# Edge attention of a graph network: the order of copy, selection and turning inside the merged group loop

## The chip, the cores and the metric

The kernel runs on one core of one Trainium2 chip. The metric is the device time of one execution in microseconds (us), lower is better. The engines that matter here are TensorE (PE, with its weight loads PEld), VectorE (DVE), ScalarE (ACT), GpSimd (POOL), which issues the gathers, and SyncE (SP), which issues the plain transfers. They run their own instruction streams in order and wait for one another on semaphores.

## What is computed

A graph with 6250 nodes and 100000 edges, sorted by their target node, goes through four network blocks, each with a residual connection and a layer norm. The first three (a graph convolution, a mean aggregation, five edge layers with batch norm) take the first 72% of the time and are not touched. The change lies in the fourth, two attention convolutions of this form (heads H = 4, channels C = 32 each):

```
def _transformer_conv(x, src, dst, ea, Wq, bq, Wk, bk, Wv, bv, We, Ws, bs, H, C):
    q = (x @ Wq + bq).reshape(n, H, C)
    k = (x @ Wk + bk).reshape(n, H, C)
    v = (x @ Wv + bv).reshape(n, H, C)
    e = (ea @ We).reshape(-1, H, C)
    kj = k[src] + e
    vj = v[src] + e
    alpha = jnp.einsum('ehc,ehc->eh', q[dst], kj) / jnp.sqrt(jnp.asarray(C, x.dtype))
    amax = jax.ops.segment_max(alpha, dst, num_segments=n)
    p = jnp.exp(alpha - amax[dst])
    denom = jax.ops.segment_sum(p, dst, num_segments=n)
    w = p / denom[dst]
    msg = (vj * w[..., None]).reshape(-1, H * C)
    out = jax.ops.segment_sum(msg, dst, num_segments=n)
    return out + x @ Ws + bs
```

## The kernel before

**Groups.** The edges are laid out in tiles of 128 that each belong to one window of 128 target nodes. Four tiles are a group (`GROUP`), and there are 208 groups (`GROUPS`) in a convolution. Rings of four buffers (`RING`) hold gathered rows, index columns and selection matrices; buffer `g` is group `q` modulo 4. Every loop is written with four groups in its body. `_converse` is the function that the change touches; it runs twice, once in each convolution, and `_attend` finishes the last 64 groups after it.

**Two jobs.** For each group the kernel (a) scores its edges and (b), later, adds its weighted messages to their targets. Job (a), "look", goes through these steps, written here with their lines:
- `index` (ScalarE, L701 to L704) copies the source numbers of a group into `idx`. It waits until the group four back has been scored (`joined`) and its value half has been written to DRAM (`spilled`).
- GpSimd (L692) issues four indirect DMAs, one for each tile, that gather the rows of keys and values into `gbuf` (`bigDE`). SyncE stores the value half to DRAM (L649, `walk_value`).
- `select` (ScalarE, L706 to L712) draws the 0/1 matrices that say which edge has which target in the window: four `Abs` (L709) and one `Relu` (L712). It waits until the group four back has been asked.
- `turned_to` (TensorE, L798) transposes the four matrices into PSUM (`turned`, two buffers).
- the copy (ScalarE, L721) brings them back to SBUF (`turn`, two buffers).
- `ask` (TensorE, L807) multiplies them with the queries of the window, which gives each edge its target's query in PSUM (`part`, two buffers). Ahead of it TensorE loads four window numbers into registers (L563).
- VectorE: `tell` (L886), `multiply` (L891, waits for the gather), `reduce` (L896), `finish` (L901).

**Job (b)** starts once a span of groups has been scored and the maxima of its softmax are known. The spans are 40, 48, 56 and 64 groups long (`SPANS`). For a group `p` of the span before:
- SyncE loads its values back (L655, `walk_value` to `rings`); `blend` (VectorE, L923) multiplies them with the weights into `msg`.
- `extend` (ScalarE, L734 and L735) puts two more sets of columns beside them. It waits for the scatter of the group two before its own.
- the marks, which edge has which target, are drawn by ScalarE for even groups (`draw`, L726 and L729) and by VectorE for odd ones (`mark`, L912).
- `scatter` (TensorE, L822) multiplies marks and messages, in two halves; VectorE adds the results to the nodes (`add`, L932).

**Stages of `_converse`.** Looking at span 0 alone (40 groups). Then, for each k = 1, 2, 3: eight "fresh" groups (`FRESH`), each a look and then a part of the serial softmax work of span k - 1 (`soft_part`, small steps that pass between VectorE, TensorE and ScalarE); then the merged loop, in which each step looks at a group of span k and adds a group of span k - 1: 40, 48 and 56 steps. Here the names in one step q are: it looks at group q and scatters group q' = q - SPANS[k].

**The order in one merged step** is written by hand, engine by engine. ScalarE: `extend` for q' + 1, then `look` (`index` for q + 2, `select` for q + 1, the copy for q), then on even groups `draw` for q' + 2. TensorE: `turned_to` q, `ask` q, `scatter` q'. VectorE: `tell`, `multiply`, and then `reduce`, `finish`, `mark` and `blend` for q' + 1 between the four adds. `_hold` is a wait; `Gate.at(n)` is the semaphore's value after n events.

Of the kernel before, what the change touches and what calls it, by code (L numbers as in the profile page):

```python
# [19 lines left out]
GROUP = 4  # L20
# [552 lines left out]
def _converse(c, table, query, agg, odd, score, spill, dram, x, skip, offset, spare, weights=()):  # L573
# [65 lines left out]
    with nc.psum_tensor(c.name("part"), [P, 2, GROUP, 2 * P], F32) as part, \  # L639
# [59 lines left out]
        def _(e):  # L699
# [14 lines left out]

            def look(i, g):
                q = i * RING + g
                index(i + (g + 2) // RING, (g + 2) % RING)
                select(q + 1, (g + 1) % RING)
                _hold(e, c.product, q - 1, c.tick_act)
                e.wait_ge(c.turned.sem, c.turned.at(q + 1))  # L720
                e.activation(turn[:, g % 2, :, :], turned[:, g % 2, :, :], ACT.Copy).then_inc(c.message.sem, 1)  # L721

            def draw(q, g):
                e.wait_ge(c.scattered.sem, c.scattered.at(2 * (q - RING + 1)))
# [33 lines left out]
            for q in range(2):  # L758
                index(0, q)
            select(0, 0)  # L760
            with _loop(e, *rounds(0)) as i:
                for g in range(RING):
                    look(i, g)
            for k in range(1, last + 1):
                begin, end = rounds(k)
                for n in range(FRESH):
                    look(begin + n // RING, n % RING)
                    soft_part(k - 1, n)
                if k == 1:
                    draw(0, 0)  # L770

                def steps(i, final):
                    for g in range(RING):
                        q = i * RING + (g - SPANS[k])
                        if not (final and g == RING - 1):
                            extend(k - 1, q + 1, (g + 1) % RING)
                        look(i, g)
                        if g % 2 == 0:
                            draw(q + 2, (g + 2) % RING)
                e.wait_ge(c.lined.sem, c.lined.at(step(k, 0)))  # L780
                extend(k - 1, STARTS[k - 1], 0)
                with _loop(e, begin + FRESH // RING, end - 1) as i:
                    steps(i, False)
                steps(end - 1, True)
# [7 lines left out]
        def _(e):  # L792
# [59 lines left out]
            def skipped(chunks):  # L852
                for n in chunks:
                    e.wait_ge(c.chunked.sem, c.chunked.at(n - 3))
                    e.matmul(skips[:, n % 4, 0:CHUNK], c.W3[:, c.parts[3]:c.parts[3] + D],
                             x[:, n * CHUNK:(n + 1) * CHUNK], start=True, stop=True).then_inc(c.applied.sem, 1)
            with _loop(e, *rounds(0)) as i:
                for g in range(RING):
                    turned_to(i, g)
                    ask(i, g)  # L860
            for k in range(1, last + 1):
                begin, end = rounds(k)
                for n in range(FRESH):
                    turned_to(begin + n // RING, n % RING)
                    ask(begin + n // RING, n % RING)
                    soft_part(k - 1, n)
                with _loop(e, begin + FRESH // RING, end) as i:
                    for g in range(RING):
                        turned_to(i, g)
                        ask(i, g)  # L870
                        scatter(i - SPANS[k] // RING, g)
            soft_part(last, 0)
            e.wait_ge(c.joined.sem, c.joined.at(GROUPS))
# [8 lines left out]
        def _(e):  # L882
# [194 lines left out]
                steps(end - 1, True)  # L1077
            for n in range(FRESH):
                soft_part(last, n)
    for gate in (c.product, c.turned, c.joined, c.message, c.scored):  # L1080
        gate.passed(GROUPS)
    c.keyed.passed(2 * GROUPS)
    c.select.passed(GROUPS + 1)
    c.near.passed((GROUPS + 1) * GROUP)
    c.index.passed(GROUPS + 2)
    for g in c.gathered:
        g.passed(16 * GROUP * ROUNDS)
# [1240 lines left out]
```

## Time and profile before

| What | us |
| --- | --- |
| median of 3 runs | 11971.59 |
| lowest and highest | 11969.77, 11971.92 |
| the profiled execution's own time | 11962.17 |
| its span in the profile | 11960.3 |

Busy over the whole span: PE 74%, PEld 56%, DVE 63%, ACT 53%, POOL 64%. In the last 12 of the page's 40 slices, which hold the two attention convolutions, PE, DVE, ACT and POOL are each busy between 30 and 70% of the time, and none of them is the plain bound. The reader should not ask there which engine has the largest share, but which wait ends last in a step. The mean granted TensorE clock is 0.851 of full speed for the whole kernel and lower in the convolutions, where it moves between its two levels, 1.2 and 2.4 GHz.

### The profile page before, as it was taken

To read this page: it belongs to the slowest core of one execution; us is meant where nothing else is said; L and a number is where in the kernel's file an instruction comes from. 1 tells how busy PE (TensorE), PEld (TensorE's weight loads), DVE (VectorE), ACT (ScalarE), POOL (GpSimd) and SP (SyncE) were. 2 spreads that over 40 slices of the span, in tenths; PEclk is the share of its full clock that TensorE was granted. 3 is DMA by queue.
4 is the path that set the end of the run, shared out by engine and by line. 5 is a ranking of instruction groups with operands and counts; after the bars stand their busy time and mean duration, and the time that the engine had idled before them with its cause. 6 is when DMAs were issued, how large, how long until landed. Compare 5 with 4: busy or idle time off the path is not lost. (4 is left out here: it accounts for less than half of the span.)

```text
span 11960.3 us, 289382 instructions
## 1 busy us (share of the span) xinstructions
PE 8826.2 (74%) x56131; PEld 6641.4 (56%) x56132; DVE 7580.9 (63%) x21898; ACT 6379.7 (53%) x16860; POOL 7683.9 (64%) x7879
## 2 busy tenths in 40 slices
PE   5887788788688868877886888688755555555555
PEld 2776677466455545555564555455445555445554
DVE  5777777555567767666766676667644445544446
ACT  4544444544455555555555555555555555455554
POOL 2777777677677757757775775677365554565553
PEclk7998899799799989998998999899866667666677
DMA  2111111222244434434443443444254444454443
GB/s 56 32 31 33 34 31 29 65 56 56 73 111 111 109 97 110 111 91 116 111 111 94 110 111 83 125 110 112 85 155 140 144 140 126 124 149 141 140 144 100
DMA packets 1311535, 1169.02 MB, mean 98 GB/s; under 512 B 239258, under 2 KB 1106238, under 8 KB 1310224
## 3 DMA queue, kind: packets, MB, share of 16 engines
q0 software_dynamic: 272544, 566.00, 18.5%
q1 hardware_dynamic: 1038256, 596.28, 17.3%
q14 instruction: 647, 5.30, 0.1%
q8 instruction: 88, 1.44, 0.1%
HBM read 1009.04 MB, written 152.40 MB: 97 GB/s over the span
## 5 line engine op out<-in xcount | busy, mean ns | idle before, releaser
L1407 POOL DMA_INDIRECT rings<-rows_key,idx x4536 | 4365.3, 962 | 1908.7 <-issue 1330.4
L1591 DVE TENSOR_TENSOR bigDE<-bigDE,part 128x128 f32 (+1 forms) x6656 | 1891.8, 284 | 1390.1 <-PE part L1502 408.9
L692 POOL DMA_INDIRECT bigDE<-rows_key_value,idx x1664 | 1627.9, 978 | 1343.4 <-ACT idx L704 731.4
L1502 PE MATMUL part<-rings 128*128 128x128 f32 (+1 forms) x11920 | 1713.3, 290 | 648.2 <-ACT rings L1443 248.0
L1515 PE MATMUL wide<-bigDE,bigC 128*128 128x384 bf16 x10800 | 1943.3, 337 | 250.3 <-DVE bigC L1573 238.8
L1502 PEld LDWEIGHTS part<-rings 128*128 128x128 f32 (+1 forms) x11920 | 1560.6, 190 | 821.7 <-issue 743.7
L1434 ACT ACTIVATE rings<-iota,relK 128x128 f32<-128x128 f32 x5960 | 1900.3, 389 | 4.9 <-issue 1.5
L1407 POOL DMA_INDIRECT rings<-rows_hidden,idx x1424 | 1377.8, 968 | 595.7 <-issue 408.7
L1426 ACT COPY idx<-srcK 128x4 int32 (+1 forms) x1490 | 283.6, 191 | 2498.8 <-PE part L1502 2324.4
L1515 PEld LDWEIGHTS wide<-bigDE,bigC 128*128 128x128 bf16 x10800 | 1069.5, 101 | 984.4 <-issue 390.0
L807 PE MATMUL part<-bigB,rings 128*128 x3328 | 741.1, 390 | 1076.0 <-ACT rings L721 1072.4
L1573 DVE TENSOR_SCALAR bigC<-bigC,node 128x512 bf16<-128x512 int16 x4410 | 1384.2, 379 | 45.1 <-issue 42.5
L807 PEld LDWEIGHTS part<-bigB,rings 128*128 128x128 f32 x3328 | 625.0, 277 | 1220.5 <-issue 1220.5
L1515 PE MATMUL wide<-bigF,bigC 128*128 128x384 bf16 x6840 | 1169.7, 326 | 174.6 <-DVE bigC L1573 172.1
L1437 ACT ACTIVATE rings<-rings,ones 128x512 f32<-128x512 f32 x1490 | 1075.6, 722 | 48.4
L1541 DVE TENSOR_TENSOR rings<-rings 128x512 f32<-128x512 f32 x945 | 654.6, 693 | 650.1 <-DMA rings<-rows_key,idx 624.7
L1515 PEld LDWEIGHTS wide<-bigF,bigC 128*128 128x128 bf16 x6840 | 654.3, 98 | 615.0 <-issue 204.0
L1515 PE MATMUL wide<-bigDE,rings 128*128 128x192 bf16 x9408 | 898.0, 253 | 108.4 <-DVE rings L1573 104.4
L1515 PEld LDWEIGHTS wide<-bigDE,rings 128*128 128x128 bf16 x9408 | 801.3, 101 | 176.6 <-issue 162.5
L886 DVE TENSOR_TENSOR bigDE<-part,wK 128x16 f32<-128x16 f32 x416 | 72.6, 175 | 1208.6 <-PE part L807 1208.5
L1573 DVE TENSOR_SCALAR rings<-W,node 128x512 bf16<-128x512 int16 x2352 | 743.4, 381 | 35.0 <-issue 34.9
L1443 ACT ACTIVATE rings<-rings 128x512 f32<-128x512 f32 x945 | 586.0, 620 | 316.8 <-DVE rings L1541 314.1
(372 smaller groups left out, 11296.6 us busy)
## 6 DMA issues: line engine op xcount, KB each, us to landing
rings<-in_attr SPq DMA_DIRECT2D x3780, 64.0 KB
walk_value<-bigDE SPq DMA_DIRECT2D x416, 256.0 KB, 2.5
rings<-walk_value SPq DMA_DIRECT2D x416, 256.0 KB
rings<-rows_key,idx POOLq DMA_INDIRECT x4536
bigDE<-rows_key_value,idx POOLq DMA_INDIRECT x1664
bigF<-in_attr SPq DMA_DIRECT2D x380, 64.0 KB
rings<-rows_hidden,idx POOLq DMA_INDIRECT x1424
rows_key<-rings SPq DMA_DIRECT2D x60, 320.0 KB, 2.6
```

The source lines that it names most:

```text
L692: e.indirect_dma_start(gbuf[:, g, r, :], None, table, bass.IndirectOffsetOnAxis(ap=c.idx[:, g, r:r + 1], axis=0)).then_inc(c.gathered[g].s ...
L807: done = e.matmul(part[:, g % 2, r, 0:D + HEADS], turn[:, g % 2, r, :], query[:, bass.ds(where[r] * (D + HEADS), D + HEADS)], start=True, ...
L1407: e.indirect_dma_start(to[:, r, 0:width], None, table, bass.IndirectOffsetOnAxis(ap=idx[:, r:r + 1], axis=0)).then_inc(gate.sem, 16)
L1426: e.copy(to, c.srcK[:, bass.ds(q_of(i, n) * GROUP, GROUP)]).then_inc(c.index.sem, 1)
L1434: e.activation(to[:, r, :], c.iota[:, :], ACT.Abs, bias=c.relK[:, bass.ds(q * GROUP + r, 1)], scale=-1.0).then_inc(c.near.sem, 1)
L1437: e.activation(to, to, ACT.Relu, bias=c.ones[:, 0:1], scale=-1.0).then_inc(c.select.sem, 1)
L1443: e.activation(x, x, ACT.Relu).then_inc(c.message.sem, 1)
L1502: last = e.matmul(part[0:width, bank(n), r, :], msg[:, r, 0:width], sel[:, r, :], start=True, stop=True)
L1515: last = e.matmul(wide[:, r, 0:3 * width], hot[:, r * P:r * P + P], room.pieces(s, 1).rearrange("p a j f -> p (a j f)"), start=s == 0, sto ...
L1541: e.tensor_tensor(to, to, plus, ALU.add).then_inc(c.joined.sem, 1)
L1573: e.tensor_scalar(hots[(half * NODE_TILES + s) % depth], room.sources[half], c.node[:, s:s + 1], None, ALU.is_equal).then_inc(c.hot.sem, 1)
L1591: e.tensor_tensor(into, into, got, ALU.add).then_inc(c.added.sem, 1)
```

## The change

In `_converse` alone:
- ScalarE: in `look` the copy of group q comes first; after it `index` for q + 2 and then `select`, which is now for q + 2 where it was for q + 1. Before the first loop there is one more `select`, for group 1. In a merged step the whole `look` now stands ahead of `extend`.
- TensorE: turning runs one group ahead. Group 0 is turned before the first loop; then every step is `ask` q, `turned_to` q + 1, and after that the soft part or the scatter.
- The counts that the semaphores have reached at the end grow by one: one group more is turned, and one group more is selected, at the end.

```
             def look(i, g):
                 q = i * RING + g
-                index(i + (g + 2) // RING, (g + 2) % RING)
-                select(q + 1, (g + 1) % RING)
                 _hold(e, c.product, q - 1, c.tick_act)
                 e.wait_ge(c.turned.sem, c.turned.at(q + 1))
                 e.activation(turn[:, g % 2, :, :], turned[:, g % 2, :, :], ACT.Copy).then_inc(c.message.sem, 1)
+                index(i + (g + 2) // RING, (g + 2) % RING)
+                select(q + 2, (g + 2) % RING)
...
             select(0, 0)
+            select(1, 1)
...
                         q = i * RING + (g - SPANS[k])
+                        look(i, g)
                         if not (final and g == RING - 1):
                             extend(k - 1, q + 1, (g + 1) % RING)
-                        look(i, g)
                         if g % 2 == 0:
                             draw(q + 2, (g + 2) % RING)
...
+            def following(i, g):
+                turned_to(i + (g + 1) // RING, (g + 1) % RING)
+            turned_to(0, 0)
             with _loop(e, *rounds(0)) as i:
                 for g in range(RING):
-                    turned_to(i, g)
                     ask(i, g)
+                    following(i, g)
...
                 for n in range(FRESH):
-                    turned_to(begin + n // RING, n % RING)
                     ask(begin + n // RING, n % RING)
+                    following(begin + n // RING, n % RING)
                     soft_part(k - 1, n)
                 with _loop(e, begin + FRESH // RING, end) as i:
                     for g in range(RING):
-                        turned_to(i, g)
                         ask(i, g)
+                        following(i, g)
                         scatter(i - SPANS[k] // RING, g)
...
-    for gate in (c.product, c.turned, c.joined, c.message, c.scored):
+    for gate in (c.product, c.joined, c.message, c.scored):
         gate.passed(GROUPS)
+    c.turned.passed(GROUPS + 1)
     c.keyed.passed(2 * GROUPS)
-    c.select.passed(GROUPS + 1)
-    c.near.passed((GROUPS + 1) * GROUP)
+    c.select.passed(GROUPS + 2)
+    c.near.passed((GROUPS + 2) * GROUP)
```

ScalarE's row in the last round of the first merged loop, where it stands without register instructions, before. L734 and L735 are `extend`, L704 `index`, L709 and L712 `select`, L721 the copy:

```order
L734 COPY bigC<-bigF 128x4x4
L735 COPY bigC<-bigC 128x4x4
L704 COPY idx<-srcK 128x4
L709 ACTIVATE rings<-iota,relK 128x128 x4
L712 ACTIVATE rings<-rings,ones 128x512
L721 ACTIVATE rings<-turned 128x512
L726 ACTIVATE rings<-iota,relK 128x128 x4
L729 ACTIVATE rings<-rings,ones 128x512
```

The same step of the changed kernel; L719 is the copy here:

```order
L719 ACTIVATE rings<-turned 128x512
L704 COPY idx<-srcK 128x4
L709 ACTIVATE rings<-iota,relK 128x128 x4
L712 ACTIVATE rings<-rings,ones 128x512
L734 COPY bigC<-bigF 128x4x4
L735 COPY bigC<-bigC 128x4x4
L726 ACTIVATE rings<-iota,relK 128x128 x4
L729 ACTIVATE rings<-rings,ones 128x512
```

The copy went from the sixth place to the first, and `extend` from the first to the fifth, ahead of `draw` (L726, L729).

TensorE's row in the first merged loop before, from the turning of a group (L798) over the loading of the window numbers (L563) to the first matmul of `ask` (L807), and then from its last to the scatter (L822):

```order
L798 MATMUL turned<-ident,rings 128x128 x4
L563 ISA
L563 TENSOR_LOAD nRow
L186 REGISTER_ALU
L805 REGISTER_ALU
L807 ISA
L807 MATMUL part<-bigB,rings 128x132
...
L820 ISA
L822 MATMUL halves<-bigC,rings 128x136 x2
L820 REGISTER_ALU
L822 MATMUL halves<-bigC,rings 128x136 x2
```

The same place in the changed kernel, from the last matmul of `ask` (L808 here) over the turning (L799) and the scatter (L823) to the loading of the next window numbers:

```order
L808 MATMUL part<-bigB,rings 128x132
L186 REGISTER_ALU
L797 REGISTER_ALU
L799 MATMUL turned<-ident,rings 128x128 x4
L186 ISA x2
L186 REGISTER_ALU
L821 ISA
L823 MATMUL halves<-bigC,rings 128x136 x2
L821 REGISTER_ALU
L823 MATMUL halves<-bigC,rings 128x136 x2
L563 ISA
L563 TENSOR_LOAD nRow
```

Turning moved from ahead of `ask` to between `ask` and the scatter, and what it turns is the next group.

## Rows read from the trace of the kernel before

**Rows 1.** Busy time by stage; columns: stretch, length, engines' busy time, clock, DMA

```profile
core 0: us, PE busy (x) PEld busy (x) DVE busy (x) ACT busy (x) POOL busy (x), PEclk, DMA share, GB/s
8656.50:8849.00 192.50, 98.60 (x464) 84.31 (x464) 68.62 (x161) 102.34 (x273) 145.12 (x155) 0.65 0.60 163
8904.80:9186.50 281.70, 171.05 (x799) 154.66 (x798) 134.72 (x381) 151.88 (x451) 154.76 (x159) 0.70 0.50 146
...
sum 2037.90, PE 1229.13 PEld 1112.76 DVE 965.46 ACT 1098.52 POOL 1088.76; mean PE 204.86 PEld 185.46 DVE 160.91 ACT 183.09 POOL 181.46
...
9186.50:9250.40 63.90, 29.58 (x121) 24.04 (x122) 32.60 (x78) 26.71 (x72) 37.24 (x35) 0.54 0.45 129
...
sum 367.70, PE 174.58 PEld 142.77 DVE 191.97 ACT 163.49 POOL 226.37; mean PE 29.10 PEld 23.79 DVE 32.00 ACT 27.25 POOL 37.73
```

**Rows 2.** Timeline of one merged step and a half, in order of time

```profile
start us, us, engine line op out<-in xcount [idle before <-releaser]
9331.85 0.20 ACT L734 COPY bigC<-bigF 128x16 f32 x1 [4.12 <-PE halves L822]
9332.33 0.19 ACT L704 COPY idx<-srcK 128x4 int32 x1
9333.33 0.94 POOL L692 DMA_INDIRECT bigDE<-rows_key_value,idx  x1 [2.21 <-ACT idx L704]
...
9334.48 0.58 ACT L721 ACTIVATE rings<-turned 128x512 f32<-128x512 f32 x1
9334.95 1.26 ACT L726 ACTIVATE rings<-iota,relK 128x128 f32<-128x128 f32 x4
...
9335.43 2.12 PE L807 MATMUL part<-bigB,rings 128*128 x8 [3.29 <-ACT rings L721]
9336.25 0.72 ACT L729 ACTIVATE rings<-rings,ones 128x512 f32<-128x512 f32 x1
9337.35 2.02 PE L822 MATMUL halves<-bigC,rings 128*128 128x136 f32 x8
9339.16 1.06 PE L798 MATMUL turned<-ident,rings 128*128 128x128 f32 x4
9339.49 0.20 ACT L734 COPY bigC<-bigF 128x16 f32 x1 [2.52 <-PE halves L822]
```

**Rows 3.** Who waited for whom in the first merged loop, 40 steps

```profile
engine line waited for: us in total, times, longest us
DVE bigDE L886 <- PE part L807: 128.8, 41, 4.2
PE part L807 <- ACT rings L721: 109.6, 40, 3.3
POOL bigDE L692 <- ACT idx L704: 86.2, 38, 2.9
```

**Rows 4.** Timeline of the looking stage without merged work

```profile
8747.46 0.19 ACT L704 COPY idx<-srcK 128x4 int32 x1 [2.35 <-DMA walk_value<-bigDE]
8748.51 0.94 POOL L692 DMA_INDIRECT bigDE<-rows_key_value,idx  x1 [0.30 <-issue]
8749.76 0.94 POOL L692 DMA_INDIRECT bigDE<-rows_key_value,idx  x1 [0.30 <-issue]
...
8753.87 0.69 DVE L891 TENSOR_TENSOR bigDE<-bigDE,part 128x512 f32<-128x512 f32 x1 [0.93 <-DMA bigDE<-rows_key_value,idx]
```

**Rows 5.** Timeline of VectorE's operations beside GpSimd's gathers, merged and fresh

```profile
9340.61 0.68 DVE L923 TENSOR_TENSOR bigC<-rings,bigF 128x512 f32<-128x512 f32 x1
9340.91 1.20 POOL L692 DMA_INDIRECT bigDE<-rows_key_value,idx  x1 [2.90 <-ACT idx L704]
...
9207.22 1.82 DVE L935 TENSOR_TENSOR_SCAN bigF<-bigF,small,bigC 128x768 f32<-128x768 f32 x1
...
9207.75 2.04 POOL L692 DMA_INDIRECT bigDE<-rows_key_value,idx  x1 [0.30 <-ACT idx L704]
```

**Rows 6.** Timeline of fresh groups of span 2, and who waited there

```profile
9190.66 1.06 PE L798 MATMUL turned<-ident,rings 128*128 128x128 f32 x4
...
9194.35 2.12 PE L807 MATMUL part<-bigB,rings 128*128 x8 [2.62 <-ACT rings L721]
...
DVE bigDE L886 <- PE part L807: 25.1, 8, 9.1
```

More of the change, by code:

```diff
@@ L716, in look @@
                 q = i * RING + g
-                index(i + (g + 2) // RING, (g + 2) % RING)
-                select(q + 1, (g + 1) % RING)
                 _hold(e, c.product, q - 1, c.tick_act)
@@ L721, in look @@
                 e.activation(turn[:, g % 2, :, :], turned[:, g % 2, :, :], ACT.Copy).then_inc(c.message.sem, 1)
+                index(i + (g + 2) // RING, (g + 2) % RING)
+                select(q + 2, (g + 2) % RING)
             def draw(q, g):
@@ L760, in _ @@
             select(0, 0)
+            select(1, 1)
             with _loop(e, *rounds(0)) as i:
@@ L774, in steps @@
                         q = i * RING + (g - SPANS[k])
+                        look(i, g)
                         if not (final and g == RING - 1):
                             extend(k - 1, q + 1, (g + 1) % RING)
-                        look(i, g)
                         if g % 2 == 0:
@@ L856, in skipped, with following @@
                              x[:, n * CHUNK:(n + 1) * CHUNK], start=True, stop=True).then_inc(c.applied.sem, 1)
+            def following(i, g):
+                turned_to(i + (g + 1) // RING, (g + 1) % RING)
+            turned_to(0, 0)
             with _loop(e, *rounds(0)) as i:
                 for g in range(RING):
-                    turned_to(i, g)
                     ask(i, g)
+                    following(i, g)
             for k in range(1, last + 1):
@@ L863, in _ @@
                 for n in range(FRESH):
-                    turned_to(begin + n // RING, n % RING)
                     ask(begin + n // RING, n % RING)
+                    following(begin + n // RING, n % RING)
                     soft_part(k - 1, n)
@@ L868, in _ @@
                     for g in range(RING):
-                        turned_to(i, g)
                         ask(i, g)
+                        following(i, g)
                         scatter(i - SPANS[k] // RING, g)
@@ L1079, in _ @@
                 soft_part(last, n)
-    for gate in (c.product, c.turned, c.joined, c.message, c.scored):
+    for gate in (c.product, c.joined, c.message, c.scored):
         gate.passed(GROUPS)
+    c.turned.passed(GROUPS + 1)
     c.keyed.passed(2 * GROUPS)
-    c.select.passed(GROUPS + 1)
-    c.near.passed((GROUPS + 1) * GROUP)
+    c.select.passed(GROUPS + 2)
+    c.near.passed((GROUPS + 2) * GROUP)
     c.index.passed(GROUPS + 2)
```

## The prediction

> **What bounds the kernel now.** First I cut the two convolutions into stages by the busy-time view [rows 1]. The six merged loops (40, 48 and 56 steps, twice) last 2037.90 us for 288 steps, 7.08 us a step. The six fresh stages last 367.70 us for 48 groups. In the plain looking stage a group takes about 5 us. No engine fills a merged step: from the first loop's row, per step, PE is busy 171.05 / 40 = 4.3 us, DVE 3.4, ACT 3.8, POOL 3.9. So a chain of waits sets the 7.08 us, and the timeline shows it [rows 2]. The scatter ends and releases ScalarE at 9331.85; ScalarE does `extend`, index, selection and then the copy (L721 at 9334.48, 0.58 us); TensorE has waited 3.29 us for that and asks at 9335.43; the scatter follows at 9337.35 and releases ScalarE at 9339.49. That is 7.64 us once around, at the lower TensorE clock. Of it 3.58 us (9331.85 to 9335.43) is ScalarE's part, in which TensorE stands still after its turning; the rest is ask 1.92, scatter 2.02 and 0.12 to the next row. The waits say the same in sums [rows 3]: TensorE waited for the copy 109.6 us in 40 steps, 2.74 each; VectorE for the ask 128.8; GpSimd 86.2 for an index column, 2.2 each, since index stands behind the same release.
>
> **The change, part by part.**
>
> *The copy ahead of index, selection and extend.* Group q is now turned before the scatter of the step ahead, so the copy finds its input early. What lay between scatter and ask, 3.58 us, leaves the path: the copy runs beside the scatter, and the ask needs only the scatter's end and a copy done before. Index and selection (together 9332.33 to 9334.48, 2.15 us) stay on ScalarE but are wanted one step later (the turning of q + 2 is in the next step). What is queued behind the copy's wait: index, select, extend, draw. `extend` still waits for the scatter of the step before, and behind it in ScalarE's queue are `draw` on even groups (L726 and L729, 9334.95 to 9336.97, 2.02) and the next copy. That is the one chain left between the two: 0.12 + 0.48 (extend, 9331.85 to 9332.33) + 2.02 + 0.58 + 0.37 = 3.6 us from a scatter's end to an ask, in the worst step. At the lower clock TensorE works longer than that between a scatter's end and the next scatter's end, and at the higher one the chain spans two steps, so it doesn't bind.
>
> *What is late next.* Each engine's own work in a step, run without a stop. TensorE at the lower clock [rows 2]: ask 1.92, scatter 1.81 (9337.35 to 9339.16), turning 0.85 (its 1.06 less the tail that overlaps): 4.6 us; less at the higher one. ScalarE: 9331.85 to 9334.48, 2.63, the copy to the next operation 0.47, and half a draw 1.01: 4.1 us. VectorE: 3.4 busy plus the gaps between dependent adds, at most 4.3. GpSimd: four gathers of 0.94 with 0.30 of issue between them (8748.51 to 8749.76 is 1.25 [rows 4]): 5.0 us. So GpSimd is the next bound. The looking stage shows that it can run so: there every gather follows the last after 0.30, though ScalarE waits 2.35 us for a store before each index column [rows 4], because index is two groups ahead. A merged step keeps that lead: from index column to gather start is 1.0 us (9332.33 to 9333.33), four gathers take 5.0, landing some 2 more, 8 us in all, and the multiply that wants them is two steps, 10 us or more, behind.
>
> *The hold on GpSimd.* A gather that starts while VectorE runs a certain kind of operation is stretched: beside L923 it took 1.20 instead of 0.94 and ended 0.82 after L923 did (9340.61 + 0.68 + 0.82 = 9342.11 = 9340.91 + 1.20); beside the scan L935 it took 2.04 and ended 0.75 after it [rows 5]. Now the idle time of GpSimd hides this; with GpSimd as the bound it counts. A step has one L923 and, every second time, one mark L912 of the same size, 0.68. A start comes each 1.25 us, falls into an operation with chance 0.68 / 1.25 = 0.54 and is held half of it, 0.34: 0.19 for each operation, 0.28 a step. The ends are 0 (starts fall beside them) and 0.82 (mark and blend together, 1.29 us, held in full every second step, half a blend in the others). I take 0.28, because the stretched rows now lie between the ends too. Hence 5.28 us a step, between 5.0 and 5.8. The Trainium skill, page "SBUF — State Buffer", section "Who interferes with whom", agrees that a VectorE operation with two SBUF inputs blocks GpSimd's reads, but infers that such a tensor_tensor does not stall descriptor generation; by that the step would be 5.0 and the sum 81 us lower. The row of 1.20 us speaks against the inference, so I don't take it.
>
> *Merged loops:* 288 x 5.28 = 1521 against 2038: **-517 us** (5.0: -598; 5.8: -367).
>
> *Turning ahead in the fresh stages.* There TensorE comes out of a soft part, turns (9190.66), waits 2.62 for the copy and asks at 9194.35 [rows 6]; with the matrices already turned and copied it asks where it now turns, up to 3.7 us earlier. VectorE waits 25.1 us for asks in a stage; the longest, 9.1, is mostly softmax work on ScalarE that stays (I count 2 of it for index and selection), and in the others the part caused by turning and copy is 1 to 3 us. I take 11 us of the 64 in a stage, 66 for six; 78 if all others go; 40 if GpSimd, whose eight groups need 8 x 5 = 40 us and more under scans [rows 5], binds first, as it may in the two stages of 55 us. **-66 us.**
>
> *Looking stages:* nothing, they are GpSimd's already [rows 1, 4]. *Added work:* one selection (2.0 us) before and one behind the loops, and one turning (0.9) before the last scatter, in each convolution. The first hides behind the first gathers, the last behind the final softmax work. I charge 2 us. More traffic in a shorter step: the DMA share, now 0.50, becomes 0.50 x 7.08 / 5.28 = 0.67, near the 0.60 at which the looking stage already runs without a pause.
>
> **Sum.** Profiled execution 11962.2 (1.9 of it outside the span) - 517 - 66 + 2 = 11381. The median of the runs lies 9.4 above the profiled one: 11391, say **11390**. Bounds: 11962 + 9 - 598 - 78 = 11295, and 11962 + 9 + 2 - 367 - 40 = 11566.
>
> **The rivals.**
> - *The chain only gets shorter.* ScalarE's row in order (extend behind the scatter, draw, copy) still stops TensorE, or registers and waits cost more than I see: for a step of 6 to 6.8 us. For it speaks that TensorE's 4.6 us leaves little slack at the lower clock. Time: 288 x (7.08 - 6.4) = 196, with half the fresh gain 33: 11742. Range 11570 to 11860.
> - *It doesn't do what it says.* If the copy always waited for a turning that is held back by its own selection, ask would come no earlier. Against: that selection was made a step before. Time 11970.
> - *Slower: index too late.* Index is now behind the copy, and the copy waits for TensorE. If gathers land more than two steps after their index column (8 us now; with the copy's 0.6 and doubled landing still 11), VectorE waits for gathers that now are in time. It decides only when that latency passes 2 x 7.08 = 14.2 us; at 16 the step is 8.0: 288 x 0.9 = 260 us more, 12230. Against: the looking stage bears higher traffic per us with no such growth.
>
> **How the numbers follow.** Forecast 0.82 (11295 to 11566), shorter chain 0.11, no effect 0.03, slower 0.04. The range 11295 to 11570 leaves out somewhat under 0.2. A measurement here tells 0.2% (24 us) from no change. Faster by more: 0.82 + 0.11 = 0.93, less a rounding for the mildest of the chain cases: 0.92; within 0.2%: 0.04; slower: 0.04.
>
> **What would show it.** Right: merged loops of 200 to 230 us for 40 steps instead of 282; gathers with 0.30 between them and some of 1.2 to 1.6 us; no wait of TensorE for the copy of near 3 us; VectorE waiting for gathers, not for asks; ScalarE waiting at index, as in the looking stage. If instead GpSimd still waits for index columns, the chain has only been shortened; if most of the gathers are stretched, the hold is larger than I took it. If the fresh stages stay at 64, the softmax chain alone sets them. The TensorE clock doesn't enter the forecast; it would if TensorE became the bound.

## The result and the profile after

| What | us |
| --- | --- |
| changed kernel, median of 4 runs | 11327.85 |
| lowest and highest | 11314.04, 11329.24 |
| kernel before beside it, median of 4 runs | 11971.76 |
| ratio, 95% interval | 0.946 (0.9443 to 0.9476) |
| profiled execution of the changed kernel | 11327.94 (span 11326.1) |

The changed kernel is 5.4% faster, 644 us by the medians and 634 by the two profiled spans (11960.3 and 11326.1). The forecast was 11390, with 11295 to 11570 as its range: the time lies in the range, and the gain is 63 us larger than forecast.

The page of the changed kernel: busy time of each engine, and the groups of the gathers and of `ask` (busy, mean ns of one, idle time ahead of them and its cause).

```profile
PE 8557.2 (76%) x56134; PEld 6362.2 (56%) x56140; DVE 7582.3 (67%) x21898; ACT 6355.2 (56%) x16870; POOL 7714.8 (68%) x7879
...
L692 POOL DMA_INDIRECT bigDE<-rows_key_value,idx x1664 | 1647.3, 990 | 692.0 <-issue 654.3
...
L808 PE MATMUL part<-bigB,rings 128*128 x3328 | 678.2, 366 | 358.8 <-ACT rings L719 236.8
```

TensorE's idle time ahead of `ask` that is put down to the copy was 1072.4 us in all 416 groups before (109.6 of it in the 40 steps of [rows 3]). It is 236.8 us now, and only 7.1 of that lies in the six merged loops. What stands ahead of a gather is no longer a wait for an index column: 654.3 of 692.0 us is `issue`, the 0.30 us between one gather and the next.

The stages of the first convolution after, cut as in [rows 1]: looking, fresh, merged, fresh, merged. Behind them stand the sums of all six merged loops and of all six fresh stages.

```profile
core 0: us, PE busy (x) PEld busy (x) DVE busy (x) ACT busy (x) POOL busy (x), PEclk, DMA share, GB/s
8670.10:8862.60 192.50, 100.11 (x468) 86.31 (x468) 68.80 (x160) 100.92 (x272) 145.02 (x154) 0.64 0.59 162
8862.60:8916.20 53.60, 31.66 (x128) 26.66 (x129) 29.24 (x65) 31.46 (x86) 41.60 (x40) 0.50 0.57 163
8916.20:9113.80 197.60, 132.55 (x786) 114.84 (x784) 135.43 (x380) 146.75 (x442) 150.07 (x153) 0.86 0.70 202
9113.80:9170.60 56.80, 32.46 (x133) 27.12 (x134) 32.95 (x76) 28.62 (x79) 42.29 (x40) 0.52 0.57 160
9170.60:9408.40 237.80, 162.38 (x948) 140.12 (x946) 162.63 (x456) 179.40 (x537) 181.01 (x186) 0.83 0.70 203
...
sum 1430.60, PE 949.40 PEld 822.62 DVE 970.63 ACT 1062.99 POOL 1086.84; mean PE 158.23 PEld 137.10 DVE 161.77 ACT 177.17 POOL 181.14
...
sum 331.40, PE 175.97 PEld 146.83 DVE 191.97 ACT 174.77 POOL 252.10; mean PE 29.33 PEld 24.47 DVE 31.99 ACT 29.13 POOL 42.02
```

Against [rows 1]: merged loops 2037.9 to 1430.6, 607.3 less, 4.97 us a step where it was 7.08; fresh stages 367.7 to 331.4, 36.3 less; the looking stage 192.5 both times. GpSimd's busy time in the merged loops did not change (1088.8 and 1086.8): it is the same work, packed into less time, 76% of it. TensorE's fell from 1229 to 949 with a granted clock of 0.83 to 0.87 where it was 0.70 in the first row.

Nearly the whole gain stands in one row, that of the gathers (busy, mean ns | idle ahead of them). These are the 832 gathers of the first convolution, the kernel before first and the changed one second. Each row also holds 73 us of idle time ahead of the first gather.

```profile
L692 POOL DMA_INDIRECT bigDE<-rows_key_value,idx x832 | 814.6, 979 | 660.0 <-ACT idx L704 366.4 <-issue 293.5
...
L692 POOL DMA_INDIRECT bigDE<-rows_key_value,idx x832 | 822.9, 989 | 334.5 <-issue 313.2 <-ACT idx L704 21.2
```

Busy and idle together are 1474.6 us before and 1157.4 after: 317.2 less. From the first gather to the last, the second convolution is 315.0 us shorter (1397.7 and 1082.7). The two make 632 us. From the last gather to the last multiplication it is another 6 and 5 us shorter (10.5 before, 4.4 and 5.1 after), and 13 are lost ahead of the first gather (8641.8 before, 8655.0 after), where the change touches nothing: 631 of the 634 us between the spans. A run of 208 groups without a pause, 5.0 us each (1.25 a gather [rows 4]), would be 1040 us; the changed kernel needs 1084: 1040, 37 of stretched gathers, 8 of pauses. In the kernel before the pauses are 334 us, counted in the same way.

The timeline of a merged step and a half of the changed kernel. L895 is `multiply`, L905 `finish`, L916 `mark`, L927 `blend`, L719 the copy.

```profile
9299.84 0.69 DVE L916 TENSOR_TENSOR rings<-relK,iota 128x512 f32<-128x512 f32 x1
...
9300.31 1.04 POOL L692 DMA_INDIRECT bigDE<-rows_key_value,idx  x1 [0.30 <-issue]
9300.81 0.69 DVE L927 TENSOR_TENSOR bigC<-rings,bigF 128x512 f32<-128x512 f32 x1 [0.28 <-DMA rings<-walk_value]
...
9302.15 0.19 ACT L704 COPY idx<-srcK 128x4 int32 x1 [1.26 <-DVE bigF L905]
...
9302.47 0.34 SPq L655 DMA_DIRECT2D rings<-walk_value  x1
...
9303.79 2.12 PE L808 MATMUL part<-bigB,rings 128*128 x8 [0.81 <-issue]
...
9306.44 0.69 DVE L927 TENSOR_TENSOR bigC<-rings,bigF 128x512 f32<-128x512 f32 x1 [2.50 <-DMA rings<-walk_value]
9306.66 1.29 POOL L692 DMA_INDIRECT bigDE<-rows_key_value,idx  x1 [0.30 <-issue]
9306.77 0.57 SPq L649 DMA_DIRECT2D walk_value<-bigDE  x1
9306.80 0.60 ACT L719 ACTIVATE rings<-turned 128x512 f32<-128x512 f32 x1 [0.36 <-PE turned L799]
```

TensorE asks (9303.79) without waiting for a copy; in [rows 2] it had waited 3.29 us. ScalarE waits at its index column, and GpSimd doesn't wait at all. Who waited for whom in the second merged loop of 48 steps, and, in the last row, the same for SyncE's own queue:

```profile
PEld halves L823 <- DVE bigDE L936: 68.3, 45, 3.2
PE halves L823 <- DVE bigDE L936: 55.1, 44, 3.0
POOL bigDE L692 <- issue: 54.7, 178, 0.7
DVE bigC L927 <- DMA rings<-walk_value: 52.2, 42, 2.5
ACT idx L704 <- DVE bigF L905: 34.8, 30, 2.6
...
SPq L649 <- DMA bigDE<-rows_key_value,idx: 170.6, 47, 5.7
```

In this stage no compute engine waits for a gather directly. SyncE does, 170.6 us of 237.8: its store of a group waits for that group's gathers, and the reload of values for the scatter (L655) stands behind the store in the same queue. By the trace's landing events the gathers of one group were in at 9306.61; the store went out at 9306.77, the reload behind it at 9307.60, and its data were in at 9311.40; the next `blend` started at 9311.67. VectorE waits for the reload, TensorE's scatter for VectorE's adds. This is how a late gather reaches the other engines. It doesn't show by itself that GpSimd sets the pace. In the second merged loop of the kernel before (342.4 us), where GpSimd was not the bound, SyncE waited for gathers even longer:

```profile
SPq L649 <- DMA bigDE<-rows_key_value,idx: 270.0, 48, 7.5
```

What names GpSimd is its own row: 8 us of pauses in 1084.

### The profile page after: what moved, and what is told of

The parts are those of the page before. It is cut to its first block and busy times, and to the rows that moved or that the text cites. A ratio compares the mean times of both kernels' runs of the same rounds, so it can differ in the third digit from the quotient of the medians.

```text
span 11326.1 us, 289319 instructions
## 1 busy us (share of the span) xinstructions
PE 8557.2 (76%) x56134; PEld 6362.2 (56%) x56140; DVE 7582.3 (67%) x21898; ACT 6355.2 (56%) x16870; POOL 7714.8 (68%) x7879
## 5 line engine op out<-in xcount | busy, mean ns | idle before, releaser
L692 POOL DMA_INDIRECT bigDE<-rows_key_value,idx x1664 | 1647.3, 990 | 692.0 <-issue 654.3
L1439 ACT ACTIVATE rings<-iota,relK 128x128 f32<-128x128 f32 x5960 | 1900.2, 389 | 4.9 <-issue 1.5
L808 PE MATMUL part<-bigB,rings 128*128 x3328 | 678.2, 366 | 358.8 <-ACT rings L719 236.8
L808 PEld LDWEIGHTS part<-bigB,rings 128*128 128x128 f32 x3328 | 583.1, 260 | 454.3 <-issue 453.7
L709 ACT ACTIVATE rings<-iota,relK 128x128 f32<-128x128 f32 x1680 | 536.5, 390 | 0.0
```

Of the source, the lines that this page charges most:

```text
L692: e.indirect_dma_start(gbuf[:, g, r, :], None, table, bass.IndirectOffsetOnAxis(ap=c.idx[:, g, r:r + 1], axis=0)).then_inc(c.gathered[g].s ...
L709: e.activation(c.sel[:, g, r, :], c.iota[:, :], ACT.Abs, bias=c.relK[:, bass.ds(q * GROUP + r, 1)], scale=-1.0).then_inc(c.near.sem, 1)
L808: done = e.matmul(part[:, g % 2, r, 0:D + HEADS], turn[:, g % 2, r, :], query[:, bass.ds(where[r] * (D + HEADS), D + HEADS)], start=True, ...
L1439: e.activation(to[:, r, :], c.iota[:, :], ACT.Abs, bias=c.relK[:, bass.ds(q * GROUP + r, 1)], scale=-1.0).then_inc(c.near.sem, 1)
```

## The experiments

Two theories were to be told apart. **GpSimd's run**: once the copy no longer stands behind the scatter, a convolution lasts as long as 832 gathers of 1.25 us, their holds and pauses. **The shorter chain**: the order of the engines still sets the step, only with fewer links. Under each kernel stands its row of the 832 gathers of the first convolution. Busy and idle in it add up to a sum that is 1157.4 for the changed kernel; twice the difference is what the first theory gives for the kernel's time.

### ScalarE's part alone, TensorE's part alone

The first kernel turns a group right ahead of its `ask`, as before, and keeps the rest of the change:

```
+                    turned_to(i, g)
                     ask(i, g)
-                    following(i, g)
                     scatter(i - SPANS[k] // RING, g)
```

> The changed kernel, but TensorE turns a group right ahead of its ask, as before; only ScalarE's new order is kept. Theory (GpSimd is the new bound, and both halves of the change were needed at the lower TensorE clock only): behind a scatter's end now stand turning 0.85, copy 0.6, two hand-overs of 0.15 and 0.37, ask 1.9 and scatter 1.8, 5.7 us a merged step at 1.2 GHz and under 5.0, GpSimd's time, at 2.4 GHz: 5.1 to 5.7 us a step, 11350 to 11550 us in all. Rival (turning ahead is what gives the gain): merged steps stay near 7 us and the time near 11970.

Measured: 11357.97 us, ratio 0.9493 (0.9477 to 0.9509), in the range of the theory.

The second keeps TensorE's part and gives ScalarE its old order:

```
                         q = i * RING + (g - SPANS[k])
-                        look(i, g)
                         if not (final and g == RING - 1):
                             extend(k - 1, q + 1, (g + 1) % RING)
+                        look(i, g)
...
             def look(i, g):
+                index(i + (g + 2) // RING, (g + 2) % RING)
+                select(q + 1, (g + 1) % RING)
...
-                index(i + (g + 2) // RING, (g + 2) % RING)
-                select(q + 2, (g + 2) % RING)
```

> The changed kernel, but ScalarE does extend, index, select (one ahead) and copy in the order of before; only TensorE turns ahead. Theory: nothing is gained in the merged loops, since the copy still stands behind extend, index and select, which stand behind the scatter; and the turning, which was hidden while TensorE waited, now stands between ask and scatter: 7.1 to 7.9 us a step, 11950 to 12220 us in all. Rival (turning was on the path): 6.2 us a step, 11700.

Measured: 12179.45 us, ratio 1.018 (1.0163 to 1.0197), in the range of the theory. The gathers of the first kernel and of the second, then a merged step and the first merged loop (columns as above) of the second:

```profile
L692 POOL DMA_INDIRECT bigDE<-rows_key_value,idx x832 | 823.7, 990 | 352.8 <-issue 314.7 <-ACT idx L704 38.1
...
L692 POOL DMA_INDIRECT bigDE<-rows_key_value,idx x832 | 812.9, 977 | 768.7 <-ACT idx L704 477.1 <-issue 291.6
...
9106.02 0.20 ACT L734 COPY bigC<-bigF 128x16 f32 x1 [5.32 <-PE halves L822]
...
9107.46 0.94 POOL L692 DMA_INDIRECT bigDE<-rows_key_value,idx  x1 [3.62 <-ACT idx L704]
...
9108.52 0.58 ACT L721 ACTIVATE rings<-turned 128x512 f32<-128x512 f32 x1
...
9109.52 2.12 PE L807 MATMUL part<-bigB,rings 128*128 x8 [3.65 <-ACT rings L721]
...
8903.60:9216.00 312.40, 175.18 (x793) 165.41 (x792) 134.60 (x380) 151.65 (x451) 152.29 (x159) 0.65 0.44 131
```

The gain is ScalarE's order: alone it brings 607 us (11964.8, the kernel before beside it, to 11358.0). TensorE's part alone costs 215. Its row shows why: from the scatter's release (9106.02) over `extend`, index, selection and copy to `ask` it is still 3.50 us, the same chain as in [rows 2], and the turning (9103.00 in the same trace, between `ask` and scatter) now lengthens the part that leads to the next release. A step is 7.8 us in this loop, 8.1 in the third. With ScalarE's part in place, turning ahead brings 30 us: the first kernel's gathers row is 19.1 longer, 38 in two convolutions.

### Selection one group ahead; extend first

Two links of the change taken back one at a time: `select(q + 1, ...)` in place of `select(q + 2, ...)`, and in the merged step `extend` ahead of `look` as before, with the order inside `look` left as changed.

> The changed kernel, but the selection runs one group ahead, as before, and no selection stands ahead of the first loop: copy q, index q+2, select q+1. Theory: the chain copy, index, select, turning (0.6 + 0.2 + 2.0 + 0.35 + 0.85 = 4.0 us) is shorter than GpSimd's 5.0, so the merged step stays at 5.0 and the whole within 0.3% of the changed kernel (11328). Rival (the second group of lead carries part of the gain): a step of 5.3 us or more, 11410 or more.

> The changed kernel, but ScalarE does extend ahead of look in the merged loops, as before; look itself has the copy first, and TensorE turns ahead. Theory: the copy stands behind the scatter again, but only with extend between: 0.12 + 0.48 + 0.58 + 0.37 + ask 1.92 + turning 0.85 + scatter 1.81 = 6.1 us a merged step at 1.2 GHz and 4.0 at 2.4 GHz, so GpSimd's 5.0 hides it at the higher clock: 5.1 to 6.0 us a step, 11360 to 11600. Rival (only index and selection had to leave the chain): no more than 0.2% over 11328.

Measured: 11321.59 us (0.946, 0.9444 to 0.9476), and 11332.48 us (0.9469, 0.9453 to 0.9485). Sums of their gathers rows: 1159.3 and 1163.8, so +4 and +13 us by the theory. Neither can be told from the changed kernel. For the first its theory was right. For the second the rival was right and the theory wrong: it had put the merged step at 5.1 to 6.0 us and the time at 11360 or more, and the steps are 5.00 to 5.13 us, where the changed kernel has 4.94 to 5.10. What counts is the order inside `look`: copy first, so that neither index nor selection stands between a scatter and an `ask`.

### Three gathers of four

One of a group's four gathers is left out, so a quarter of the edges are scored with stale rows. Store and `multiply` wait for three gathers then.

```
-                    for r in range(GROUP):
+                    for r in range(GROUP - 1):
                         e.indirect_dma_start(gbuf[:, g, r, :], None, table,
```

> The changed kernel with three of each group's four gathers; the fourth is left out, so a quarter of the edges are scored with stale rows. Theory (GpSimd sets the merged step and the looking stages): GpSimd needs 3.75 us a group, and the next bound comes up, TensorE and the waits around it, 3.8 to 4.5 us in a merged step; 11328 - 288 x 0.6 - 2 x 30 = about 11090 us. Rival (a chain sets the step, and GpSimd only happens to be as long): 5.0 us a step, 11300.

Measured: 10882.44 us, one execution. The first two merged loops, here of 40 and 48 steps:

```profile
8846.60:9004.30 157.70, 115.84 (x803) 99.41 (x801) 133.35 (x381) 146.51 (x455) 116.85 (x119) 0.96 0.76 227
9056.30:9243.10 186.80, 135.13 (x963) 114.58 (x961) 160.59 (x456) 176.15 (x547) 141.62 (x143) 0.99 0.77 228
```

Steps of 3.94 and 3.89 us, where three gathers of 1.25 take 3.75. Everything else in a merged step can be done in 3.9 us at the clock granted here, so in the changed kernel's 4.97 the other engines have slack, and the gathers are the bound. (At the lower clock, with the 4.6 us that the prediction counts for TensorE, the slack would be smaller.) I had expected 11090, with another engine binding at a longer step. The granted clock, 0.96 to 0.99 here, may be what took TensorE out of that; no run tested it. This run decides for GpSimd's run. It also takes traffic away, so one may ask whether the transfers were the bound and not GpSimd. They were not: with three gathers 227 and 228 GB/s are moved, at a DMA share of 0.76 and 0.77, where the changed kernel moves 202 and 203 at 0.70. The fresh stages stayed at 46 to 55 us (53 to 58 in the changed kernel): there something else holds too.

### Index one group ahead; longer fresh stages

The pipe's depth, and what VectorE's work in the fresh stages costs. In the first kernel the index column is made one group ahead; in the second VectorE has two extra reductions of some 3.3 us in each of the six fresh stages, 40 us in all.

```
-                index(i + (g + 2) // RING, (g + 2) % RING)
+                index(i + (g + 1) // RING, (g + 1) % RING)
...
                 if n == 2:
+                    if k < last:
+                        e.tensor_reduce(c.stats[:, 0, 0:24], c.iota[:, :].unsqueeze(1).to_broadcast([P, 24, P]),
+                                        AX.X, ALU.add)
```

> The changed kernel, but the index column is copied for the next group, not for the one after it, and only one stands ahead of the first loop: GpSimd's lead is one group. Theory (GpSimd runs without a stop through the whole of _converse because two groups are ready when a softmax step holds everything up): the lead, now 6 us of 10 in the merged loops, becomes about 1, GpSimd stops in the fresh stages for some 8 to 12 us each and a little in the merged loops: 11390 to 11480 us. Rival (one group of lead is enough): within 0.2% of 11328.

> The changed kernel with two more VectorE operations in each of the six fresh stages (sums over 3072 elements that nobody reads, about 3.3 us each, one in the parts 2 and 4 of the softmax work). Theory A (the fresh stages are under GpSimd too, which never waits in them; their length on VectorE is given back in the merged loop behind them): at most 10 us more than the changed kernel, 11328 to 11340. Theory B (fresh stages and merged loops add up, as the prediction counted them): 6 x 6.6 = 40 us more, 11365.

Measured: 11385.94 us (0.9512, 0.9496 to 0.9528), and 11341.1 us (0.9474, 0.9458 to 0.949). Their gathers rows, in this order:

```profile
L692 POOL DMA_INDIRECT bigDE<-rows_key_value,idx x832 | 818.2, 983 | 368.9 <-issue 311.5 <-ACT idx L704 57.5
...
L692 POOL DMA_INDIRECT bigDE<-rows_key_value,idx x832 | 818.2, 983 | 352.2 <-issue 312.6 <-ACT idx L704 39.6
```

Index one ahead costs 58 us, and the row gives 59 (1187.1 against 1157.4, twice). By the stages 39 us of it arise in the fresh stages, which are 59 to 64 us long, against 53 to 58, and 21 in the merged loops, with steps of 5.04 to 5.13. The theory's lower bound was 11390.

The second kernel is 13 us slower, 26 by the row; theory A had allowed 10 and theory B said 40. But the run tests less than it was meant to. VectorE is busy 38 us longer in the six fresh stages (230.5 against 192.0), and they are only 12.4 us longer (343.8 against 331.4), so most of the added work went into time in which VectorE had been idle. The merged loops gave nothing back; they are 15.7 us longer (1446.3 against 1430.6). Why, the lead shows, which is how many groups GpSimd has issued ahead of `multiply`. It is 1.5 at the start of a fresh stage in both kernels; at the end it is 2.75 to 3.5 in the changed kernel and 2.0 to 2.5 in this one. So a fresh stage isn't a term of its own: what it costs is what it makes GpSimd pause, and the merged loop behind it is longer or shorter by the lead that it hands over.

### The marks in another form

VectorE draws the marks of odd groups with four `tensor_scalar` in place of one `tensor_tensor`, to see whether the kind of operation holds the gathers.

```
-                e.tensor_tensor(marks[:, g, :, :], (relK, broadcast), (iota, broadcast), ALU.is_equal)
+                for r in range(GROUP):
+                    done = e.tensor_scalar(marks[:, g, r, :], c.iota[:, :], c.relK[:, bass.ds(q * GROUP + r, 1)],
+                                           None, ALU.is_equal)
```

> The changed kernel; VectorE draws the marks of odd groups with four tensor_scalar operations (one SBUF input and a scalar column each) in place of one tensor_tensor with two SBUF inputs. Theory (operations with two SBUF inputs hold a gather that starts under them): the mark's part of the stretched gathers goes, 0.15 us a merged step becomes 0.10 or less, 10 to 20 us in all: 11305 to 11320. Rival (tensor_scalar holds GpSimd as well, for as long as it runs): no fewer stretched gathers, 11325 to 11360.

> The changed kernel with both small edits: selection one group ahead, as before the change, and the marks of odd groups drawn by four tensor_scalar instead of one tensor_tensor. On a chip where GpSimd issues without a pause (gathers land some 2 us after their issue, as in the first profiles), the hold theory expects 11300 to 11320, some 10 to 15 us under the changed kernel's 11328, with holds of about 30 us in a convolution instead of 37, and the selection to make no difference. If the earlier 11315 of the marks alone was only a difference between chips, this gives 11320 to 11335 and the holds tell nothing. On a chip where gathers land some 10 us after their issue, as in the last three runs, GpSimd waits for index columns and the holds are covered: then this lies within 1% of the kernel before, 0.985 to 0.995 of it, and says nothing on the marks.

Measured: 11315.32 us (0.9451, 0.9435 to 0.9466) for the marks alone; 11320.67 us (11298.91 to 11322.12; 0.9453, 0.9441 to 0.9466) with selection one ahead as well. The first, then the second:

```profile
L692 POOL DMA_INDIRECT bigDE<-rows_key_value,idx x832 | 816.5, 981 | 330.9 <-issue 309.4 <-ACT idx L704 21.6
...
L692 POOL DMA_INDIRECT bigDE<-rows_key_value,idx x832 | 814.0, 978 | 332.7 <-issue 307.7 <-ACT idx L704 25.1
```

The holds go from 37 to 30 and 28 us in a convolution: busy time is 6.4 and 8.9 us lower than 822.9. By the sums of the rows alone that says little, since the two kernels of the section before have the old marks and 818.2. Over both convolutions 160 gathers are longer than 1.1 us in the changed kernel, 113 and 97 in these two, and 141 to 159 in the experiments above that have the old marks and all four gathers and take 11320 to 11390 us.

But this doesn't show that it takes two SBUF inputs to hold a gather. Of the 138 gathers that start beside a `tensor_scalar` of the new marks in the first kernel, 85 end 0.81 or 0.82 us after it, just as beside the old mark. They lose little, 0.08 us at most, because one such operation takes 0.28 us where the old mark takes 0.69. So the rival is right that `tensor_scalar` holds a gather too, and the long holds are fewer because each operation is short.

By the first theory the kernels should be some 20 us faster (sums 1147.4 and 1146.7, twice the difference to 1157.4); they are 13 and 7 us of 11328, with intervals that overlap that of the changed kernel. The profiled executions reach the first gather, up to which all these kernels are alike, anywhere between 8637 and 8659 us, so the time decides nothing of this size. A version that beats the changed kernel isn't shown by this.

### The same kernels on another chip

Three kernels (the changed one, with the new marks, with both edits) ran on another chip, on which the kernel before takes 14965.6 us.

> The changed kernel itself, run beside the next two, so that differences of 0.1% can be read on one chip: 11315 to 11330 us.

> The kernel with the marks drawn by tensor_scalar, again, beside the changed one. Theory (each operation with two SBUF inputs costs GpSimd what it holds): 10 to 15 us under the changed kernel, since the holds fell by 13 us in the first look. Rival (that was chance between executions): no difference beyond 5 us.

> The marks drawn by tensor_scalar, and the selection one group ahead as before the change. Theory (GpSimd's own time, holds and gaps are all that counts, and the second group of selection is not needed): the same as with tensor_scalar alone, within 5 us. Rival (selection two ahead is worth something): 5 us or more slower.

Measured: 14765.36 us (0.9866, 0.9848 to 0.9883), 14845.48 (0.9934, 0.9914 to 0.9954) and 14818.61 (0.9909, 0.9891 to 0.9927). The changed kernel there: its gathers row, its first looking stage (columns as above), and a piece of that stage.

```profile
L692 POOL DMA_INDIRECT bigDE<-rows_key_value,idx x832 | 823.3, 990 | 679.8 <-ACT idx L704 377.5 <-issue 302.2
...
11424.70:11677.20 252.50, 113.21 (x467) 98.33 (x468) 66.36 (x161) 100.45 (x273) 149.11 (x158) 0.56 0.45 127
...
11515.40 1.06 PE L799 MATMUL turned<-ident,rings 128*128 128x128 f32 x4
...
11521.22 0.60 ACT L719 ACTIVATE rings<-turned 128x512 f32<-128x512 f32 x1 [6.11 <-remote]
11521.29 0.17 DVE L890 TENSOR_TENSOR bigDE<-part,wK 128x16 f32<-128x16 f32 x1 [9.82 <-remote]
...
11521.72 0.18 ACT L704 COPY idx<-srcK 128x4 int32 x1
...
11522.71 0.95 POOL L692 DMA_INDIRECT bigDE<-rows_key_value,idx  x1 [4.01 <-ACT idx L704]
```

All three expectations failed. They were worked out for the other chips, and the order of the three kernels isn't the one expected either: the new marks are 80 us slower here than the old ones, with intervals that don't meet, and no run shows why.

A gather takes the same 0.95 us there, and the engines' busy times are alike, but a looking group takes 6.3 us, not 4.8, and a merged step 7.0, not 4.97. GpSimd waits for index columns 377.5 us in a convolution again, and the change is worth 1.3%. The part of the kernel that the change doesn't touch is slower too: the first gather starts at 11409.5 us, not at 8655.0.

The expectation of the marks with both edits, above, says that gathers land some 10 us after their issue on this chip. That was my reading of the time from the end of a group's fourth gather to its `multiply`: the median is 10.7 us in the looking stage, where it is 2.0 in the changed kernel's first profile, and 12.6 in the merged loops against 3.9. It is a wrong reading, since `multiply` waits for more than the rows. In the merged loops of the kernel before, on the first chip, the same time is 13.4 to 13.9 us, and there the rows had landed 1.8 us after the fourth gather. On the slow chip, wherever GpSimd pauses long enough to tell, the last packet of a group's gathers ends 1.5 us after the fourth gather in the looking stage and 1.9 to 2.0 in the merged loops; before the change, on the first chip, it was 1.5.

What is seen to come late there are hand-overs between engines. In the piece shown ScalarE's copy waits for TensorE's `ask` and turning alone. The turning ends at 11515.40 + 1.06 = 11516.46, its semaphore counts it at 11521.20, and the copy starts at 11521.22. In that stage the copy finds ScalarE idle ahead of it in 39 of 40 groups and starts 2.2 us, by the median, after the end of the turning; in the changed kernel's first profile ScalarE is idle ahead of it in 4 groups of this stage, and the copy starts within 0.1 us. The ends of matmuls in a profile are modelled, so it may also be that TensorE itself ended later than its rows say. What makes the copy late stays open, and with it what bounds the step on this chip. All comparisons of kernels above are from the chips on which the kernel before takes 11965 to 11972 us.

## Why the prediction was right, and where it was off

**The bound before, and what released it: right.** The chain of scatter, ScalarE's four steps and `ask` set the step. With ScalarE's order put back the 3.50 us from release to `ask` return, and the step is 7.8 us.

**The next bound, GpSimd: right.** Three gathers in place of four took the step to 3.9, with more traffic per us than before, and GpSimd pauses for 8 and 5 us in the changed kernel's two convolutions. The shorter chain as a rival is out: at the clock granted in that run nothing else needs more than 3.9.

**The hold: mis-sized.** I took 0.28 us a step; measured are 0.12 to 0.19 in the six loops, 0.15 on average. The rule itself stands: 9306.44 + 0.69 + 0.82 = 9307.95 = 9306.66 + 1.29, and beside the mark 9299.84 + 0.69 + 0.82 = 9301.35 = 9300.31 + 1.04. But a gather needs 0.94 anyway, so beside one of these operations it is late by what remains of it less 0.12, not by all that remains: a start in the first 0.56 us (chance 0.56 / 1.25 = 0.45) loses 0.28 on average, 0.125 for each operation, 0.19 a step. The Trainium skill, page "SBUF — State Buffer", section "Who interferes with whom", infers that a tensor_tensor of two SBUF inputs doesn't stall descriptor generation; here both rows are of that kind and both gathers are stretched, so the measurement decides against the inference, though the price is smaller than I took it.

**Merged loops: -517 forecast, -607 measured; fresh stages: -66 forecast, -36 measured.** The failed step is the adding up. I summed the stages as if each had a bound of its own. GpSimd knows no stages: in the fresh ones it gathered on almost without pause (252 of 331 us busy, most of the rest its 0.30 gaps), was stretched there by 0.4 to 0.8 us a group, and gained up to two groups on the others, which the merged loops gave back as steps of 4.94 to 5.10 us, below the 5.28 that I had summed. From gather to gather GpSimd's own step in the merged loops is 5.17 to 5.20 us. Of the 90 us that the loops gave beyond the forecast, 36 are the smaller hold (288 times 0.13), and some 53 are this lead: 1.7 groups of 5.2 us in each of six loops. In the fresh stages I had counted on the 11 us a stage that the earlier `ask` would free; 6 came. The right sum is over the convolution: 1040 of gathers, 37 of holds, 8 of pauses, 1084 instead of 1400, twice: 632 us, and 12 for the shorter ends. By terms, against 581 forecast: 90 more in the loops, 30 less in the fresh stages, together 644, and 10 lost elsewhere between the two profiled executions give 634.

**Looking stages and added work: right.** 192.5 us both times. The 13 us lost ahead of the first gather are no effect of the change: over the experiments' profiles that gather starts between 8637 and 8659.

**Index late: didn't happen here.** The lead from index column to first gather grew to 6.1 us on average in the merged loops, from 0.9. With index one group ahead it is 2.6, and the kernel is 58 us slower. The rival's own condition, rows that land more than two steps after their index column, arose in no run: on the slow chip too the last packets of a group's gathers end some 2 us behind the fourth gather. So its price and its threshold of 14.2 us stay untested.

**What would show it: three of five, and a fourth nearly.** Seen were gathers 0.30 apart, some of them 1.0 to 1.46 us long; no wait of 3 us for the copy; ScalarE waiting at index. The loops of 40 steps took 197.6 and 198.7 us, just under the 200 to 230 named. VectorE waits not for gathers but for the reload of values, which stands in SyncE's queue behind a store that waits for them. I hadn't followed that queue, and the wait looks like another bound until one asks what the reload waited for. DMA share: 0.67 forecast, 0.68 to 0.70 measured.

## What to carry to other kernels

When a chain between engines is cut, ask which engine can then run without a pause, and sum its instructions, holds and pauses over the whole region, not stage by stage: an engine with buffers ahead carries its lead from one stage into the next. Check each half of a change for what it does alone: work moved ahead of time on one engine only pays when what waited for it was also moved, and costs when the chain it now stands in is the bound. A wait for a plain transfer may be a wait for whatever its queue holds ahead of it.

## What the runs showed of the hardware

- Chips differ, and not only by a factor: the same program takes 11970 us on some and 14966 on one, with the same 0.95 us for a gather and 1.5 to 2.0 us from the fourth gather to the last packet, against 1.5, but with TensorE's turning counted 4.7 us after its end in the piece shown. What a change is worth differs as well: 5.4% and 1.3%.
- TensorE's granted clock in the first merged loop was 0.65 at 7.8 us a step (TensorE's part alone), 0.70 at 7.04 (before), 0.86 at 4.94 (changed) and 0.96 at 3.94 (three gathers). It is no such order everywhere: the changed kernel's six fresh stages, all of 53 to 58 us for eight groups, have 0.50 to 0.76.
- A gather that starts beside a VectorE operation of 128x512 elements with both inputs in SBUF (0.69 us), with more than 0.13 us of it left, ends 0.81 or 0.82 us after that operation: 122 of 122 beside `mark` and 128 of 130 beside `blend` in the changed kernel. Of the 255 that start beside `multiply`, which is of the same size and takes one input from PSUM, none is stretched beyond 1.1 us, and of the 197 beside `reduce` (one input) none.
- A gather beside a `tensor_scalar` of 128x128 elements (0.28 us, one SBUF input and a scalar column) is held as well: 85 of 138 end 0.81 or 0.82 us after it, the longest of these 85 at 1.03 us. The 38 that start at about the same moment as it does are not.
- A gather that starts beside one of the long scans of the softmax (1.5 to 2.1 us) ends 0.75 or 0.76 us after it: 24 of 24 in the changed kernel and 24 of 24 before, up to 2.74 us long.
